# A log-polar convolution with batch norm: the second half's m1 weights summed by a chain of adding transfers

## What is computed

```python
xp = log_pooling(x)                                   # B, C, 4*28, 3*28
out = conv(xp, w_conv1, stride=(4, 3)) + conv(x, w_center) + b_center
mean, var = out.mean(axis=(0, 2, 3)), out.var(axis=(0, 2, 3))
out = (out - mean) * rsqrt(var + 1e-5) * gamma + beta
return relu(out + x)
```

## Time and profile before

| | |
|---|---|
| median of 3 runs | 1605.91 us (1605.81 to 1606.45) |
| the profiled execution | 1605.88 us |
| its span, first to last instruction | 1604.1 us |
| mean granted clock of TensorE, of full speed | 0.958 |
| PE busy | 1458.2 us (91%), 8518 matmuls |
| DVE busy | 1474.4 us (92%), 1512 instructions |
| ACT busy | 760.6 us (47%) |
| POOL busy | 122.6 us (8%) |
| queue of POOL's transfers | 82.45 MB, 28.4% of 16 engines' span |
| SP's queue | 89.32 MB, 15.2% |

### The profile page before, as it was taken

One profiled execution on the slowest core, in us unless ns is written; L12 is line 12 of the kernel. 1 busy time (PEld: TensorE's weight loads), 2 busy tenths in 40 slices (PEclk: granted clock), 3 DMA queues, 4 the chain that ended last, 5 costly groups with the idle time before them and its releaser, 6 DMA issues.

```text
span 1604.1 us, 22797 instructions
## 1 busy us (share of the span) xinstructions
PE 1458.2 (91%) x8518; PEld 1456.1 (91%) x8518; DVE 1474.4 (92%) x1512; ACT 760.6 (47%) x853; POOL 122.6 (8%) x155
## 2 busy tenths in 40 slices
PE   9899999999999999999999999999999999995000
PEld 9899999999999999999999999999999999995000
DVE  8999999999999999999999999999999999996731
ACT  4345555445444554445444554445444554444632
POOL 1000000000000000000000000000000000000100
PEclk9999999999999999999999999999999999998555
DMA  6244443344333443344333443344334444569999
GB/s 170 69 80 88 84 94 81 80 94 84 81 80 74 85 93 81 80 94 84 81 80 74 87 92 82 80 94 84 83 79 77 87 89 103 155 198 380 419 425 398
DMA packets 46632, 197.55 MB, mean 123 GB/s; under 512 B 5536, under 2 KB 5536, under 8 KB 46624
## 3 DMA queue, kind: packets, MB, share of 16 engines
q0 software_dynamic: 20736, 82.45, 28.4%
q1 hardware_dynamic: 21024, 89.32, 15.2%
q10 hardware_dynamic: 4864, 25.69, 3.9%
HBM read 147.67 MB, written 49.77 MB: 123 GB/s over the span
## 4 chain that ended last, share of the span: by engine, by line
PE 86%; DVE 4%; ACT 4%; ACTq 3%; issue 1%; DMA 0%; DVEq 0%
PE acc L772 29%; PE acc L774 29%; PE acc L773 29%; ACTq L509 3%; ACT phase L506 2%; ACT phase_rest L506 2%; DVE phase_rest L514 1%; DVE pooled_split L515 1%; DVE d L514 0%; DVE inner_split L515 0%; DVE y_stage L514 0%; ACT unread L451 0%; ACT x_pad L506 0%; DMA x_pad<-x 0%; ACT w_inner L392 0%
## 5 line engine op out<-in xcount | busy, mean ns | idle before, releaser
L418 ACT ACTIVATE pooled_split<-phase_rest 128x1456 fp32r<-128x1456 f32 x192 | 273.0, 1422 | 595.5 <-DVE phase_rest L514 595.5
L515 DVE TENSOR_TENSOR pooled_split<-phase_rest,pooled_split 128x1456 fp32r<-128x1456 f32 x192 | 317.8, 1669 | 0.0
L772 PE MATMUL acc<-pooled_split,w_first_outer 128*128 128x364 f32 x768 | 253.8, 330 | 1.1 <-DVE pooled_split L515 1.1
L772 PE MATMUL acc<-pooled_split,w_outer 128*128 128x364 f32 x768 | 252.2, 328 | 1.5 <-DVE pooled_split L515 1.4
L774 PE MATMUL acc<-pooled_split,w_outer 128*128 128x364 f32 x768 | 252.7, 329 | 0.0
L773 PE MATMUL acc<-pooled_split,w_first_outer 128*128 128x364 f32 x768 | 252.5, 329 | 0.0
L773 PE MATMUL acc<-pooled_split,w_outer 128*128 128x364 f32 x768 | 252.5, 329 | 0.0
L774 PE MATMUL acc<-pooled_split,w_first_outer 128*128 128x364 f32 x768 | 252.3, 328 | 0.0
L772 PE MATMUL acc<-inner_split,w_inner 128*128 128x392 f32 (+1 forms) x640 | 215.8, 337 | 2.9 <-DVE w_inner L557 2.9
L772 PE MATMUL acc<-inner_split,w_first 128*128 128x392 f32 (+1 forms) x640 | 216.8, 339 | 0.2 <-DVE inner_split L515 0.2
L773 PE MATMUL acc<-inner_split,w_inner 128*128 128x392 f32 (+1 forms) x640 | 216.6, 338 | 0.0
(11 more groups left out here) (95 smaller groups left out, 2486.1 us busy)
## 6 DMA issues: line engine op xcount, KB each, us to landing
row<-x_wide POOLq DMA_DIRECT2D x64, 558.0 KB, 5.8
ends<-x_wide POOLq DMA_DIRECT2D x64, 504.0 KB, 5.5
x_pad<-x SPq DMA_DIRECT2D x64, 392.0 KB, 3.1
y_dram<-y_stage SPq DMA_DIRECT2D x30, 784.0 KB, 3.3
out<-phase ACTq DMA_DIRECT2D x16, 784.0 KB, 28.4
phase<-y_dram SPq DMA_DIRECT2D x15, 784.0 KB, 16.7
phase_rest<-y_dram SPq DMA_DIRECT2D x14, 784.0 KB, 14.1
out<-phase_rest ACTq DMA_DIRECT2D x14, 784.0 KB, 30.0
```

What stands on the lines that cost most here:

```text
L418: nc.scalar.activation(view(pooled_split, 2 * j * PAIR, (1, PAIR)), reused_view(POOLED_LOW + 2 * j * PAIR, (1, PAIR)), ACT.Copy)\
L515: sub = lambda out_, a, b: nc.vector.tensor_tensor(out_, a, b, ALU.subtract)
L772: nc.tensor.matmul(place, hi_w, hi_in, start=start, stop=False)
```

## The change

The first half's sums are made as before. For the second half:

- The host hands over a further input, `w_side`, 128 x 3 x 768: the raw taps (d, d, a), (f, a, c) and (f, 0, c) of the second half side by side, whose sum is the side part.
- POOL, behind the first half's `row2` and `ends` sums of image 0, issues five transfers of 128 x 768 floats (384 KB) to the buffer `spare`: the first writes, the other four add (the second and third part of `w_side`, then the middle taps twice). Each of the four waits for the landing of the one before. The result is m1.
- DVE's `transform_weights(1)` waits for the fifth landing (`w_plus_ready` at 80) and makes m2 = m1 - 4 mid in one operation. Its wait for the first half's lo parts goes, as another buffer is used.
- ACT's and DVE's splits read `spare` for the second half.
- Two memsets of DVE in the first half (the edges of `d03` and of `row3v`) are done by POOL among its first ones, whose number goes from 7 to 9.

```diff
+        def w_sums(c, first, n):
+
+            return view((y_stage, spare)[c], first * CHANNELS, (1, n * CHANNELS))
...
-        ZEROED = 7
+        ZEROED = 9
...
+                    if isinstance(image, int) and c == 0:
+                        sum_weights()
+
+            def sum_weights():
+
+                parts = [w_side[:, k, :] for k in range(3)]
+                parts += 2 * [w_raw[:, 1, RAW_MID:RAW_MID + 3, :].rearrange("p k o -> p (k o)")]
+                pool.dma_start(w_sums(1, 0, 3), parts[0]).then_inc(w_plus_ready, 16)
+                for k in range(1, len(parts)):
+                    wait_first(w_plus_ready, 16 * k)
+                    pool.dma_start(w_sums(1, 0, 3), parts[k], accum_op=ALU.add).then_inc(w_plus_ready, 16)
...
-                        source = view(y_stage, 0, (1, (b - a) * CHANNELS))
+                        source = w_sums(c, 0, b - a)
...
                 dve.wait_ge(w_loaded[c][0], 16)
-                wait_from_one(dve, w_lo_ready, len(GROUPS) * c)
+                if c == 1:
+
+                    dve.wait_ge(w_plus_ready, 5 * 16)
+                    nc.vector.scalar_tensor_tensor(out=w_sums(1, 3, 3), in0=raw(RAW_MID, 3), scalar=-4.0,
+                                                   in1=w_sums(1, 0, 3), op0=ALU.mult, op1=ALU.add)\
+                        .then_inc(w_sums_ready, 1)
+                    return
...
-                nc.vector.memset(view(d03, 0, (TALL, 2 * U), (TALL - 1, 2)), 0.0)
+                if not (isinstance(image, int) and s == 0):
+                    nc.vector.memset(d_edges(), 0.0)
...
-                nc.vector.memset(row3v(-ROW3V_AT, (ROW3V_H, W + 3), (1, EDGES)), 0.0)
+                if not (isinstance(image, int) and s == 0):
+                    nc.vector.memset(row3v_edges(), 0.0)
```

More of the change, by code:

```diff
@@ L5, with conv_bn_relu_program @@
 from concourse import mybir
-def conv_bn_relu_program(nc, x, x_wide, w_raw, b_center, gamma, beta, out, y_dram):
+def conv_bn_relu_program(nc, x, x_wide, w_raw, w_side, b_center, gamma, beta, out, y_dram):
     F32 = mybir.dt.float32
@@ L132, in row3v, with d_edges, row3v_edges @@
             return reused_view(start_of["pooled_split"] + ROW3V_AT + first, *dims)
+        def d_edges():
+            return view(d03, 0, (TALL, 2 * U), (TALL - 1, 2))
+        def row3v_edges():
+            return row3v(-ROW3V_AT, (ROW3V_H, W + 3), (1, EDGES))
         def w_part(c, lo, tap):
@@ L199, in conv_bn_relu_program @@
         w_loaded = [[sem(f"w_loaded{c}{part}") for part in range(2)] for c in range(CH)]
+        w_plus_ready = sem("w_plus_ready")
         w_sums_ready = sem("w_sums_ready")
@@ L261, in _ @@
             for edge in (std[:, :], pooled_split[:, 2 * PAIR:2 * PAIR + HALF], row2[:, :], ends[:, :],
-                         x_pad[:, 0:2 * H], x_pad[:, X_PAD:X_PAD + 2 * H], x_pad[:, CH * X_PAD:]):
+                         x_pad[:, 0:2 * H], x_pad[:, X_PAD:X_PAD + 2 * H], x_pad[:, CH * X_PAD:], d_edges(), row3v_edges()):
                 if edge.dtype == F32R:
@@ L537, in transform_weights @@
                                                op0=ALU.mult, op1=ALU.add).then_inc(w_moved, 1)
-                dve.wait_ge(w_moved, 2 * c + 1)
+                dve.wait_ge(w_moved, 1)
                 nc.vector.scalar_tensor_tensor(out=view(y_stage, 0, (1, 3 * CHANNELS)), in0=raw(RAW_MID, 3),
@@ L541, in transform_weights @@
                     .then_inc(w_moved, 1)
-                dve.wait_ge(w_moved, 2 * c + 2)
+                dve.wait_ge(w_moved, 2)
                 nc.vector.scalar_tensor_tensor(out=side(0, 3), in0=raw(RAW_MID, 3), scalar=-2.0,
@@ L845 @@
     w_raw = np.ascontiguousarray(w[:, order][:, :, by_half].reshape(128, halves, len(order), channels))
+    a, c, d, f = (w_raw[:, 1, k] for k in range(4))
+    w_side = np.stack([np.concatenate(part, axis=1) for part in ((d, d, a), (f, a, c), (f, np.zeros_like(a), c))], axis=1)
     def per_partition(v):
@@ L857 @@
         "w_raw": w_raw,
+        "w_side": np.ascontiguousarray(w_side),
         "b_center": per_partition(L0_conv_b_center),
```

## The result

| | before | changed |
|---|---|---|
| median of 11 runs | 1606.29 us | 1610.52 us (1609.99 to 1611.68) |
| the profiled execution | 1605.88 us | 1610.66 us |
| its span | 1604.1 us | 1609.0 us |

The ratio is 1.0025 (95% interval 1.0018 to 1.0033), or 4.2 us longer (2.9 to 5.3). That is beyond the forecast of 1607.4 and just above the range, whose upper end was 1609.9. By the number it is rival B, to which the prediction gave 0.18.

A forecast was written before the change was run, and what follows sets the result against it. PE bounds the body, shifted by DVE's chain up to 78.45 us. The fifth landing at 38.5 us starts DVE's sum at 38.65 instead of 37.16: +1.5 on 1605.88 gives 1607.4 us, range 1604.8 to 1609.9.

The forecast's parts named there:

- rival B: POOL's chain much later, by first two links under weight loads or POOL steps over 1 us; over 3.2 us longer; chance 0.18.
- What bounds the kernel: PE bounds the body; DVE's chain reaching the `pooled_split` piece that ends at 78.45 us later or earlier shifts everything behind.
- The floor: At DVE's `w_inner` lo part: most that an early chain can gain, limited by ACT's splits; -0.95 us, rounded to -1.0 with memsets.
- The 0.13 us for the memset: DVE's first half: gain counted for both memsets given to POOL together, 0 to 0.25 us, lost if DVE waits.
- The first link: POOL's plain first transfer, issued behind `ends`: lands at 15.2 us at the earliest, 17.5 at the latest; 16.5 taken.
- The second link: POOL's second transfer, issued at 17.1 us under the weight loads: 5.1 to 8.4 us; 6.7 taken, landing at 23.2.
- The free links: Third to fifth transfers with nothing else moving: 5.1 us each, 4.5 to landing and 0.57 on POOL; 15.3 in all.
- The two-point slope: Accumulating transfers of 558 KB (5.8 us) and 504 KB (5.4 us), extended down to 384 KB: 4.5 us from issue to landing.
- The likely band for the fifth landing: Landing of POOL's fifth transfer, for which DVE's sum waits: 38.5 us forecast, 34.7 to 41.5 taken for likely.
- The page's formula: Skill page's estimate for GpSimd-issued transfers, 2.0 us plus bytes over 436 GB/s: link 2.9 us plus POOL's part; not adopted.
- The clock: PE's granted clock would stay at 1.00 throughout, while its first wait grows from 2.9 to 4.4 us.
- Behind the chain: Second half's `row` on POOL goes out at about 35 us instead of 25.34, still covered by over 1 us.

## Why the prediction was wrong

**What bounds the kernel: right.** PE's first wait, and by how much DVE's chain reaches the hand-over. A shift of 4.69 us at the sum gave 4.70 at the hand-over, and with six links it was 9.0 us at the sum and 9.4 in the time.

**The floor: right in kind, a little too large.** The prediction said -1.0 us with ACT's splits as the limit. With the wait taken away ACT was the limit, at 0.7 to 0.8 us at DVE. The 0.13 us for the memset wasn't there, as DVE waits for its own result at that place.

**The first link: its early end was the right one here.** It landed at 15.05; the prediction's earliest was 15.2, and it took 16.5. It had been issued ahead of the loads and hardly felt them. In the run with three transfers the same one landed at 16.3, so a part of this term is what one execution happens to give.

**The second link is the step that failed.** "5.1 us to 8.4; I take 6.7". From landing to landing it was 10.1 us, 9.55 and 0.52 on POOL: 3.4 more than taken and 1.7 above the upper bound. The bound was the excess of the x load, 5.5 us for 392 KB. That load was the second of four that SP issued, and what was queued behind it did not hold it up. The transfer of the chain was issued behind all four. What that meant can be read from the packets of the two queues, q1 being SP's and q0 POOL's (packets, MB, share of the 16 engines), from its issue at 15.61 to 19.6 us and then from 19.6 to 24.7:

```profile
q1 hardware_dynamic: 351, 1.62, 99.3%
...
q1 hardware_dynamic: 667, 1.04, 59.5%
q0 software_dynamic: 144, 0.39, 40.5%
```

For 4.0 us the engines moved nothing of the transfer, only loads; the third transfer, issued with no load in the way, has its first packet after 1.6 us. From then on both queues moved side by side. So the transfer did not wait for the end of the loads; it began while they still ran, and they took longer in return: the last weight load took 12.0 us instead of 9.3. The prediction had the loads over by about 23 us, while SP's last packet of this phase came at 25.8 (22.8 before).

A row of the trace before that answers to such a place is the last of the weight loads, issued at about 13 us, which the prediction didn't show (KB, us to landing):

```profile
w_stage<-w_raw SPq DMA_DIRECT2D x1, 768.0 KB, 9.3
```

It is 9.3 us: with that as its price the sum would have come out 3.2 us higher, at 1610.6. That it fits so closely is partly luck, as it is a plain load of twice the bytes. The other runs bear the place out: with the loads released later the third transfer had the delay (8.3 us, its first packet 4.3 us after issue; the second 5.5); with all of them at the start the first `row` sum and the chain's first transfer had it; and a plain copy at the same place took 7.9 us, its first packet 3.8 us after issue.

**The free links: 5.1 us taken, 5.3, 5.6 and 5.7 measured.** The two-point slope gave 4.5 us from issue to landing, the trace has 4.8 to 5.1 (and the run with six links 4.5 to 4.8); POOL's part was 0.52 against 0.57. Over three links it is 1.3 us. So the terms are: first link -1.45, second +3.4, the other three +1.3, together +3.2 on a forecast of +1.5, which makes the 4.7 us of the profiled executions. The likely band for the fifth landing, "34.7 to 41.5", has a slip in its upper end: 17.5, 8.4 and three links of 5.4 make 42.1. The landing, at about 41.7, lies inside that, though the second link alone went past its bound, because the first came early: two errors that partly cancel.

**Rival B.** Its condition came true, a fifth landing behind 40.2, but half of its mechanism did not. The weight loads were the cause, by the second link alone; POOL's step from landing to issue was 0.52 us, not over 1, and the sign that the prediction gave for B, issues over 6 us apart from 24 us on, did not appear (5.3 and 5.6).

**The page's formula.** By the Trainium skill ("DMA: Bandwidth & Descriptors", "Anatomy of one DMA — SWDGE (gpsimd) path") a transfer of 384 KB is, as an estimate, 2.9 us. The plain copies in the empty stretch took 3.4 to 3.8, not far above it; the additions there took 4.5 to 5.3, and what was issued behind queued loads 8 to 10. The formula has a term for the bytes and none for an addition or for loads of another queue, and the rows were the right thing to hold to. The x load against which the prediction held it is issued by SP and not on that path, so its 3.1 us were no test of it.

**The clock.** "The granted clock 1.00 throughout" was wrong. It fell to 0.50, and the 1.4 us that this cost fell into a wait of 1.4 us that PE had left behind it. The prediction had not counted on this cover; that the time shows nothing of the clock is luck.

**Behind the chain: right.** The second half's `row` went out at 37.22 (foreseen: about 35) instead of 25.34 and landed at 46.5, ahead of DVE's use at 48.60. No wait on it appeared, though the cover was 2.1 us.

What stays open is how the engines choose between the queues: the traces show that a transfer issued behind the loads gets nothing for 3.8 to 4.3 us (the first `row` sum behind all loads: 4.5) and then a share beside them, not by what rule. Why the clock fell behind 2.1 us of waiting in one kernel and not behind 2.9 in another is open as well.

## What to carry to other kernels

A chain in which each transfer waits for the one before pays the whole latency per link, so count the links against the time at which the result is due, and price each at the place where it is issued: one that is issued behind queued loads got no packet for 4 us here and then had to share with them, and its nearest row was the last of those loads, not one in their midst. Here three links were in time and five were not, and one link issued 3 us earlier repaired the five. Operations taken from an engine are worth only what the next wait on that engine leaves: of 2.1 us only 0.8 reached PE.

## What was not expected of the hardware

- An addition during a transfer of 384 KB costs 1.3 to 1.4 us over the plain copy from the same queue in an empty stretch (4.8 to 5.1 us against 3.4 to 3.8; over all runs such additions took 4.5 to 5.3), and 1.6 us where the transfer stands behind loads (9.55 against 7.9).
- A transfer of POOL's queue issued at 15.61 us, behind loads of SP's queue, had its first packet 4.0 us later, with the engines 99% busy on the loads; from there both queues moved side by side.
- TensorE's granted clock fell to 0.50 in an idle time of 7.6 us; the first matmuls behind it ran at that level, and from 50 us on it was at 1.00. In the run with the first transfer ahead it was down behind a wait of 2.1 us.
- Taking a 0.16 us memset from between two dependent operations of VectorE gained nothing: a wait of 0.19 us for the engine's own result stood in its place. Two of its other waits for its own results, at 8.40 and 9.39 us of the kernel before, leave 0.03 to 0.04 us; why this one is longer isn't shown.
